# A recommendation tower on one core: the fold of its first layer's weights is moved from the start into the first chunk, in five steps

## The chip, the cores and the metric

The kernel runs on one core of one Trainium2 chip. The metric is the device time of one execution in microseconds.

## The reference

For each of 2048 samples, 32 table rows of 64 numbers are looked up and stacked. Every one of the 496 pairs of fields gives one number, a bilinear form with a matrix of its own; a linear layer takes the 496 numbers to 256, and a small network of three layers follows. All is float32.

```python
e = jnp.stack([tbl_0[ids[:, 0]], ..., tbl_31[ids[:, 31]]], axis=1)   # 2048 x 32 x 64
rows, cols = np.triu_indices(32, k=1)
pij = jnp.einsum('bpe,dpe,bpd->bp', e[:, rows, :], kernel, e[:, cols, :])
z = pij @ W.T + b                                                   # 2048 x 256
h = jnp.concatenate([z, dense_ctx], axis=1)                         # + 16 columns
h = jnp.maximum(h @ W_top1 + b_top1, 0.0)                           # 512
h = jnp.maximum(h @ W_top2 + b_top2, 0.0)                           # 256
y = h @ W_top3
```

## The kernel before

**The fold.** Nothing nonlinear lies between `W` and `W_top1`, so the kernel multiplies the two once and applies the product to the pair sums: `w_comb = W.T @ W_top1[:256]`, and likewise `b_comb = W_top1[:256].T @ b + b_top1`. This is what is called the fold. It has 8 narrow products of one column, which a float32 matmul makes 16 instructions at L401, for the bias, and for each of four groups of rows two products of 128 by 512, four instructions at L406. VectorE moves the results out of PSUM: one addition at L360, and at L368 one copy for each of groups 0 and 1 and four copies of 30 rows for each of groups 2 and 3, whose remaining rows hold the weights of the dense columns. The first use of `w_comb_sb` and `b_comb_sb` is in the layers of chunk 0, which stand in the program among the slots of chunk 1.

**Chunks, turns, slots, sums, layers.** The batch is cut into chunks of 1, 3, 4, 4 and 4 tiles of 128 samples, so the moving side of a matmul is 128, 384 or 512 columns wide. In a chunk:
- GpSimd gathers table rows by indirect DMA (L280), one DMA for each field and tile, 512 in all, in the order chunk, double (a pair of neighbouring fields), field, tile. Double `j` of chunk 0 needs gathers `2j` and `2j + 1`, counted from 0.
- A *turn* transposes a double on TensorE (L431), and ScalarE copies it to `emb_t` (L316).
- A *slot* is a pair of doubles: 16 matmul instructions of 64 by 32 weights (L448) into a pair of PSUM banks, which VectorE multiplies by the other factor into `prod` (L387; L382 and L384 for slots within doubles). There are 128 slots in a chunk, two of them to a *phase*.
- A *sum* adds a quad of blocks of `prod` over partitions: 16 matmul instructions (L468), two phases behind its slots.
- Seven *layer* steps (L494) belong to the chunk before and stand among the slots, from phase 5 on.

**The order.** `program()` writes one list of steps, `PROGRAM`, by hand; every engine walks it and does its own part of each step. It begins with the fold, then the turns of doubles 0 to 3 of chunk 0, then the slots. The further turns of chunk 0 come one phase ahead of the first slot that needs them. The fold waits at its end for `s_folded_out`, that is for VectorE's last copy, before TensorE goes on.

**The ring.** Six PSUM banks are three pairs. Slots, turns and layers take them in turn, in the order of `RING_USES`; `ring_free` makes TensorE wait until the use three before has been read (by VectorE for a slot, by ScalarE for a turn or a layer). The fold writes four banks and one more directly, which is why it has to be out before the ring starts.

**Loads.** ScalarE's queue brings `w_cols` and `W_top1` (semaphore `s_factors`) and then the other weights; the SP queue brings the ids and the 8.2 MB of bilinear matrices in eight pieces. Both are issued in the first ten microseconds.

Of the kernel before, what the change touches and what calls it, by code (L numbers as in the profile page):

```python
# [10 lines left out]
D1 = 256  # L11
H1 = 512
# [42 lines left out]
PROD_BLOCKS = 16  # L55
PROD_QUADS = PROD_BLOCKS // 4
TURNS_AHEAD = 4

SPARE_AT = NQUADS - (NGROUPS - 1) * GROUP_QUADS  # L60
# [65 lines left out]

def program():

    steps = [("fold", 0, 0)]
    steps += [("turn", 0, j) for j in range(TURNS_AHEAD)]  # L130
    for i in range(NCHUNKS):
        for phase in range(NPHASES):
            steps += [("slot", i, s) for s in range(phase * PHASE, (phase + 1) * PHASE)]
            if i == 0:
                turned = [j for j in range(TURNS_AHEAD, DOUBLES) if FIRST_SLOT[j] // PHASE - 1 == phase]
            else:
                turn = TURNS_AHEAD + phase // TURN_EVERY
                turned = [turn] if phase % TURN_EVERY == TURN_EVERY - 1 and turn < DOUBLES else []
            steps += [("turn", i, j) for j in turned]
            turn = (phase - NPHASES) // TURN_EVERY + TURNS_AHEAD  # L140
            if i + 1 < NCHUNKS and phase % TURN_EVERY == TURN_EVERY - 1 and turn >= 0:
                steps.append(("turn", i + 1, turn))
            if phase < SUM_LAG and i > 0:
                late = range(quads_done(NPHASES - 1 + phase - SUM_LAG), quads_done(NPHASES + phase - SUM_LAG))
                steps += [("sum", i - 1, q) for q in late]
            done = range(quads_done(phase - SUM_LAG - 1), quads_done(phase - SUM_LAG))
            steps += [("sum", i, q) for q in done]
            k = (phase - FIRST_LAYER_PHASE) // TURN_EVERY
            if i > 0 and phase % TURN_EVERY == TURN_EVERY - 1 and 0 <= k < NOUTS:
                steps.append(("layer", i - 1, k))  # L150
    steps += [("sum", NCHUNKS - 1, q) for q in range(quads_done(NPHASES - 1 - SUM_LAG), NQUADS)]
    steps += [("layer", NCHUNKS - 1, k) for k in range(NOUTS)]
    return steps
# [2 lines left out]
PROGRAM = program()  # L156

RING_USES = [step for step in PROGRAM if step[0] in ("slot", "turn", "layer")]
RING_USE = {step: n for n, step in enumerate(RING_USES)}  # L160
TURN_USE = {step[1:]: n for n, step in enumerate(step for step in PROGRAM if step[0] == "turn")}

# [10 lines left out]
def build(nc, tables, ids, dense_t, k_slots, w_cols, l0_b, w_top1, b_top1, w_top2, b_top2, w_top3, out):  # L173
# [6 lines left out]
    with ExitStack() as ctx:  # L180
# [169 lines left out]
        @block.vector  # L350
        def _(dve):
            nc.vector.memset(ident[:], 0.0).then_inc(s_consts, 1)
            nc.vector.memset(row_sel[:], 0.0).then_inc(s_consts, 1)
            dve.wait_ge(s_consts, 2)
            nc.vector.memset(row_sel[:, 31:32], 1.0).then_inc(s_consts, 1)

            dve.wait_ge(s_factors, 16 * 4)
            dve.wait_ge(s_folded, 1)
            nc.vector.tensor_tensor(b_comb_sb[:], bilinear[:, NSUMS, 0:H1 // P], b1_sb[:], ALU.add).then_inc(s_folded_out, 1)  # L360
            for at, g in enumerate(reversed(range(NSUMS))):
                dve.wait_ge(s_folded, at + 2)
                if g >= NSUMS - HALVES:
                    parts_out = [slice(32 * b, 32 * b + SPARE_AT) for b in range(4)]
                else:
                    parts_out = [slice(0, P)]
                for rows in parts_out:
                    last = nc.vector.tensor_copy(w_comb_sb[rows, g, :], bilinear[rows, g, :])  # L368
                last.then_inc(s_folded_out, 1)

            def multiply(i, s):
                m, j = SLOTS[s]
                n = cols(i)
                g = i * NSLOTS + s
                bank = ring_bank("slot", i, s)
                quad = i * NQUADS + SLOT_BLOCK[s] // 4
                at = (i * NBLOCKS + SLOT_BLOCK[s]) % PROD_BLOCKS

                wait(dve, s_summed, quad - PROD_QUADS + 1)
                dve.wait_ge(s_bilinear, g + 1)  # L380
                if j is None:
                    nc.vector.tensor_tensor(prod[EMB:P, at, 0:n], bilinear[EMB:P, bank, 0:n],  # L382
                                            emb_t[EMB:P, m - 1, 0:n], ALU.mult)
                    last = nc.vector.tensor_tensor(prod[0:EMB, at, 0:n], bilinear[0:EMB, bank + 1, 0:n],  # L384
                                                   emb_t[0:EMB, m, 0:n], ALU.mult)
                else:
                    last = nc.vector.tensor_tensor(prod[:, at:at + 2, 0:n], bilinear[:, bank:bank + 2, 0:n],  # L387
                                                   emb_t[:, j:j + 1, 0:n].to_broadcast([P, 2, n]), ALU.mult)
                last.then_inc(s_prod, 1)

            for kind, i, which in PROGRAM:
                if kind == "slot":
                    multiply(i, which)

        @block.tensor
        def _(pe):
            def fold():
                pe.wait_ge(s_factors, 16 * 4)
                for m in range(H1 // P):
                    for k in range(D1 // P):  # L400
                        last = nc.tensor.matmul(bilinear[:, NSUMS, m:m + 1], w1_sb[:, k, m * P:(m + 1) * P],  # L401
                                                l0_b_sb[:, k:k + 1], start=k == 0, stop=k == D1 // P - 1)
                last.then_inc(s_folded, 1)
                for g in reversed(range(NSUMS)):
                    for k in range(D1 // P):
                        last = nc.tensor.matmul(bilinear[:, g, :], w_cols_sb[:, k, g * P:(g + 1) * P], w1_sb[:, k, :],  # L406
                                                start=k == 0, stop=k == D1 // P - 1)
                    last.then_inc(s_folded, 1)
                pe.wait_ge(s_consts, 3)
                pe.wait_ge(s_ident, 1)  # L410

                pe.wait_ge(s_folded_out, 1 + NSUMS)

            def ring_free(kind, i, which):

# [4 lines left out]
                if kind == "slot":  # L420
                    pe.wait_ge(s_prod, i * NSLOTS + which + 1)
                elif kind == "turn":
                    pe.wait_ge(s_emb_t, TURN_USE[i, which] + 1)
                else:
                    pe.wait_ge(s_layer_out, i * NOUTS + which + 1)

            def turn(i, j):
                ring_free("turn", i, j)
                pe.wait_ge(s_gathered[j], gathered_count(i))
                for t in range(CHUNKS[i][1]):  # L430
# [43 lines left out]
            def layer(i, k):  # L474
                n = cols(i)
                if i == 0 and k == 0:
                    pe.wait_ge(s_weights, 16 * 11)
                ring_free("layer", i, k)
                if k < H1_OUTS:
                    pe.wait_ge(s_sums_out, (i + 1) * NSUMS)  # L480
# [16 lines left out]

            for kind, i, which in PROGRAM:
                if kind == "fold":
                    fold()  # L500
                elif kind == "turn":
                    turn(i, which)
                elif kind == "slot":
# [49 lines left out]
```

## Time and profile before

| what | value |
|---|---|
| median of 3 runs | 882.09 us (881.82 to 883.49) |
| the profiled execution, its own time | 880.07 us |
| span of the profiled execution | 878.1 us |
| mean granted TensorE clock | 0.996 |
| TensorE busy | 838.8 us (96%) |
| VectorE busy | 632.9 us (72%) |
| GpSimd busy | 483.9 us (55%) |
| ScalarE busy | 71.7 us (8%) |
| fold's matmuls on TensorE | 3.6 us (L401) and 9.4 us (L406) |

### The profile page before, as it was taken

What the parts mean: (1) busy time and instruction counts of PE and PEld (TensorE: products, weight loads), DVE (VectorE), ACT (ScalarE), POOL (GpSimd) and SP (SyncE); (2) the same over time, 40 slices, a digit from 0 to 9 for tenths busy, and PEclk for the clock granted to TensorE, in tenths of its full rate; (3) what the DMA queues carried; (4) which work ended last, traced back from release to release, by engine and by line L of the source; (5) the groups of instructions that cost most, each with busy time, mean ns of one, the idle gap of its engine ahead of it and who ended that gap; (6) DMA issues with size and microseconds to landing.
All of it is one profiled execution on the core that took longest, in us unless ns stands there. A gap on an engine that the chain in (4) does not pass through costs nothing.

```text
span 878.1 us, 33839 instructions
## 1 busy us (share of the span) xinstructions
PE 838.8 (96%) x15748; PEld 346.6 (39%) x15748; DVE 632.9 (72%) x694; ACT 71.7 (8%) x136; POOL 483.9 (55%) x517
## 2 busy tenths in 40 slices
PE   5767899999999999999999999999999999999988
PEld 3545545444443333333333333333333333333333
DVE  3556676799986558999885548999875557999950
ACT  0000011100011110000011110000011111000001
POOL 6777777777777777777777777777720000000000
PEclk9899999999999999999999999999999999999999
DMA  9511111111111111111111111111100000000000
GB/s 333 185 31 30 32 29 30 30 29 31 28 30 28 28 29 28 29 28 29 29 29 29 27 28 29 29 30 28 29 13 2 1 1 2 2 3 2 2 3 0
DMA packets 21597, 29.36 MB, mean 33 GB/s; under 512 B 11121, under 2 KB 11665, under 8 KB 20945
## 3 DMA queue, kind: packets, MB, share of 16 engines
q0 software_dynamic: 16384, 16.81, 10.4%
q1 hardware_dynamic: 3394, 8.79, 2.7%
q8 instruction: 123, 2.02, 0.9%
q10 hardware_dynamic: 1680, 1.61, 0.6%
q14 instruction: 16, 0.13, 0.0%
HBM read 27.17 MB, written 0.01 MB: 31 GB/s over the span
## 4 chain that ended last, share of the span: by engine, by line
PE 94%; issue 3%; DVE 2%; DMA 1%; ACT 0%; SPq 0%; ACTq 0%; DVEq 0%
PE bilinear L448 52%; PE sums L468 26%; PE bilinear L494 11%; PE bilinear L431 4%; DVE w_comb_sb L368 1%; DMA b_sb<-b_top 1%; DVE prod L387 1%; PE bilinear L406 0%; PE bilinear L401 0%; SPq L261 0%; DMA sums_sb<-dense_t 0%; ACTq L298 0%; DVE prod L384 0%; DVE prod L382 0%; DVEq L180 0%
## 5 line engine op out<-in xcount | busy, mean ns | idle before, releaser
L387 DVE TENSOR_TENSOR prod<-bilinear,emb_t 128x1024 f32<-128x1024 f32 (+2 forms) x600 | 579.4, 1006 | 192.5 <-PE bilinear L448 185.3
L280 POOL DMA_INDIRECT emb<-table,ids_sb x512 | 483.4, 944 | 158.7 <-issue 155.3
L448 PE MATMUL bilinear<-emb_t,k_sb 64*32 64x512 f32 (+2 forms) x10240 | 523.2, 507 | 14.1 <-issue 12.0
L448 PEld LDWEIGHTS bilinear<-emb_t,k_sb 64*32 64x32 f32 x10240 | 190.2, 107 | 281.2 <-issue 250.7
L468 PE MATMUL sums<-prod,row_sel 64*32 64x512 f32 (+2 forms) x4960 | 286.6, 508 | 7.7 <-issue 7.3
L468 PEld LDWEIGHTS sums<-prod,row_sel 64*32 64x32 f32 x4960 | 88.7, 107 | 118.1 <-issue 83.0
L316 ACT ACTIVATE emb_t<-bilinear 128x512 f32<-128x512 f32 (+2 forms) x80 | 40.8, 513 | 501.5 <-PE bilinear L431 463.1
L494 PE MATMUL bilinear<-sums_sb,w_comb_sb 128*128 128x512 f32 (+2 forms) x160 | 59.8, 519 | 3.4 <-DMA sums_sb<-dense_t 1.5
L431 PEld LDWEIGHTS bilinear<-ident,emb 128*128 128x128 f32 x256 | 27.3, 141 | 53.2 <-DVE prod L387 47.8
L431 PE MATMUL bilinear<-ident,emb 128*128 128x128 f32 x256 | 45.4, 291 | 1.8 <-DVE w_comb_sb L368 1.6
L494 PEld LDWEIGHTS bilinear<-sums_sb,w_comb_sb 128*128 128x128 f32 x160 | 27.1, 190 | 36.8 <-issue 25.5
L494 PE MATMUL bilinear<-h_sb,w_sb 128*128 128x512 f32 (+5 forms) x100 | 37.6, 517 | 1.7 <-ACT h_sb L332 0.9
L382 DVE TENSOR_TENSOR prod<-bilinear,emb_t 64x512 f32<-64x512 f32 (+2 forms) x40 | 23.5, 588 | 5.8 <-PE bilinear L448 4.7
L494 PEld LDWEIGHTS bilinear<-h_sb,w_sb 128*128 128x128 f32 (+1 forms) x100 | 14.8, 168 | 26.0 <-issue 16.4
L324 ACT ACTIVATE sums_sb<-sums 128x512 f32<-128x512 f32 (+2 forms) x20 | 9.1, 509 | 192.4 <-PE sums L468 192.4
L384 DVE TENSOR_TENSOR prod<-bilinear,emb_t 64x512 f32<-64x512 f32 (+2 forms) x40 | 23.0, 576 | 0.5
L332 ACT ACTIVATE h_sb<-bilinear,b_comb_sb 128x512 f32<-128x512 f32 (+2 forms) x20 | 12.0, 602 | 61.7 <-PE bilinear L494 61.7
L401 PE MATMUL bilinear<-l_b_sb,h_sb 128*128 128x1 f32 x16 | 3.6, 353 | 8.1 <-DMA b_sb<-b_top 8.1
L406 PE MATMUL bilinear<-h_sb 128*128 128x512 f32 x16 | 9.4, 754 | 0.0
L368 DVE COPY w_comb_sb<-bilinear 30x512 f32<-30x512 f32 (+1 forms) x10 | 6.8, 687 | 3.5 <-PE bilinear L406 3.4
L336 ACT ACTIVATE h_sb<-bilinear,b_sb 128x512 f32<-128x512 f32 (+2 forms) x10 | 6.0, 602 | 32.0 <-PE bilinear L494 32.0
L360 DVE TENSOR_TENSOR b_comb_sb<-bilinear,b_sb 128x4 f32<-128x4 f32 x1 | 0.2, 163 | 10.6 <-PE bilinear L401 10.6
(12 smaller groups left out, 12.2 us busy)
## 6 DMA issues: line engine op xcount, KB each, us to landing
emb<-table,ids_sb POOLq DMA_INDIRECT x512
k_sb<-k_slots SPq DMA_DIRECT2D x2, 1088.0 KB, 11.5
k_sb<-k_slots SPq DMA_DIRECT2D x1, 1600.0 KB
k_sb<-k_slots SPq DMA_DIRECT2D x1, 1472.0 KB, 15.0
k_sb<-k_slots SPq DMA_DIRECT2D x1, 960.0 KB, 9.2
k_sb<-k_slots SPq DMA_DIRECT2D x1, 896.0 KB, 20.7
k_sb<-k_slots SPq DMA_DIRECT2D x1, 576.0 KB, 10.4
h_sb<-w_cols ACTq DMA_DIRECT2D x1, 512.0 KB, 4.0
```

The source lines that it names most:

```text
L280: nc.gpsimd.indirect_dma_start(emb[:, j, t, f % 2, :], None, tables[f], bass.IndirectOffsetOnAxis(ap=ids_sb[:, start + t, f:f + 1].bitcast ...
L316: nc.scalar.activation(emb_t[:, j, 0:cols(i)], bilinear[:, ring_bank("turn", i, j), 0:cols(i)], ACT.Copy).then_inc(s_emb_t, 1)
L332: nc.scalar.activation(h1_sb[:, k, 0:n], source, ACT.Relu, bias=b_comb_sb[:, k:k + 1]).then_inc(s_layer_out, 1)
L368: last = nc.vector.tensor_copy(w_comb_sb[rows, g, :], bilinear[rows, g, :])
L382: nc.vector.tensor_tensor(prod[EMB:P, at, 0:n], bilinear[EMB:P, bank, 0:n], emb_t[EMB:P, m - 1, 0:n], ALU.mult)
L384: last = nc.vector.tensor_tensor(prod[0:EMB, at, 0:n], bilinear[0:EMB, bank + 1, 0:n], emb_t[0:EMB, m, 0:n], ALU.mult)
L387: last = nc.vector.tensor_tensor(prod[:, at:at + 2, 0:n], bilinear[:, bank:bank + 2, 0:n], emb_t[:, j:j + 1, 0:n].to_broadcast([P, 2, n]), ...
L406: last = nc.tensor.matmul(bilinear[:, g, :], w_cols_sb[:, k, g * P:(g + 1) * P], w1_sb[:, k, :], start=k == 0, stop=k == D1 // P - 1)
L431: last = nc.tensor.transpose(bilinear[:, ring_bank("turn", i, j), t * P:(t + 1) * P], emb[:, j, t, :, :], ident[:])
L448: last = nc.tensor.matmul(bilinear[col:col + QUARTER, bank + row // EMB, 0:n], k_sb[row:row + EMB, s, col:col + QUARTER], emb_t[row:row + ...
L468: last = nc.tensor.matmul(sums[32 * b:32 * b + 32, half, 0:n], row_sel[rows, 31 - pos:63 - pos], prod[rows, at + b, 0:n], start=pos == 0, ...
L494: last = nc.tensor.matmul(bilinear[0:weights.shape[1], ring_bank("layer", i, k), 0:n], weights, x, start=term == 0, stop=term == LAYER_TER ...
```

## The change

The fold is cut into five steps, `("fold", 0, 0)` to `("fold", 0, 4)`: step 0 makes the bias, steps 1 to 4 one group of rows each (3, 2, 1, 0). They leave the head of the program and stand behind the slots of phases 9, 19, 29, 39 and 49 of chunk 0. Each is a use of the ring like a slot: it waits until its bank pair is free, writes the first bank of it, and the use three behind it waits until VectorE has copied the result. VectorE does the copies where the step stands in the program, between the products of the slots. The wait for VectorE's last copy moves to the first layer step, and the waits for the constants to the first turn.

```diff
+FOLD_EVERY = 10
...
-    steps = [("fold", 0, 0)]
-    steps += [("turn", 0, j) for j in range(TURNS_AHEAD)]
+    steps = [("turn", 0, j) for j in range(TURNS_AHEAD)]
...
+            if i == 0 and phase % FOLD_EVERY == FOLD_EVERY - 1 and phase // FOLD_EVERY <= NSUMS:
+                steps.append(("fold", 0, phase // FOLD_EVERY))
...
-RING_USES = [step for step in PROGRAM if step[0] in ("slot", "turn", "layer")]
+RING_USES = [step for step in PROGRAM if step[0] in ("fold", "slot", "turn", "layer")]
...
-            dve.wait_ge(s_factors, 16 * 4)
-            dve.wait_ge(s_folded, 1)
-            nc.vector.tensor_tensor(b_comb_sb[:], bilinear[:, NSUMS, 0:H1 // P], b1_sb[:], ALU.add).then_inc(s_folded_out, 1)
-            for at, g in enumerate(reversed(range(NSUMS))):
-                dve.wait_ge(s_folded, at + 2)
+            def fold_out(k):
+
+                dve.wait_ge(s_folded, k + 1)
+                source = bilinear[:, ring_bank("fold", 0, k), :]
+                if k == 0:
+                    nc.vector.tensor_tensor(b_comb_sb[:], source[:, 0:H1 // P], b1_sb[:], ALU.add).then_inc(s_folded_out, 1)
+                    return
+                g = NSUMS - k
...
-                    last = nc.vector.tensor_copy(w_comb_sb[rows, g, :], bilinear[rows, g, :])
+                    last = nc.vector.tensor_copy(w_comb_sb[rows, g, :], source[rows, :])
                 last.then_inc(s_folded_out, 1)
+
+            dve.wait_ge(s_factors, 16 * 4)
...
             for kind, i, which in PROGRAM:
-                if kind == "slot":
+                if kind == "fold":
+                    fold_out(which)
+                elif kind == "slot":
                     multiply(i, which)
...
-            def fold():
-                pe.wait_ge(s_factors, 16 * 4)
...
+            def fold(k):
+                ring_free("fold", 0, k)
+                bank = ring_bank("fold", 0, k)
+                if k == 0:
+                    pe.wait_ge(s_factors, 16 * 4)
...
+                else:
+                    g = NSUMS - k
+                    for part in range(D1 // P):
+                        last = nc.tensor.matmul(bilinear[:, bank, :], w_cols_sb[:, part, g * P:(g + 1) * P],
+                                                w1_sb[:, part, :], start=part == 0, stop=part == D1 // P - 1)
                 last.then_inc(s_folded, 1)
...
-                pe.wait_ge(s_consts, 3)
-                pe.wait_ge(s_ident, 1)
-
-                pe.wait_ge(s_folded_out, 1 + NSUMS)
...
+                elif kind == "fold":
+                    pe.wait_ge(s_folded_out, which + 1)
...
             def turn(i, j):
+                if i == 0 and j == 0:
+                    pe.wait_ge(s_consts, 3)
+                    pe.wait_ge(s_ident, 1)
...
                 if i == 0 and k == 0:
                     pe.wait_ge(s_weights, 16 * 11)
+                    pe.wait_ge(s_folded_out, 1 + NSUMS)
```

## Rows read from the trace of the kernel before

**Rows 1.** The page: span, busy time of TensorE, its busy tenths in 40 slices
```profile
span 878.1 us, 33839 instructions
...
PE 838.8 (96%) x15748; PEld 346.6 (39%) x15748; DVE 632.9 (72%) x694; ACT 71.7 (8%) x136; POOL 483.9 (55%) x517
...
PE   5767899999999999999999999999999999999988
```

**Rows 2.** The chain that ended last, in order of time (start us, us, what)
```profile
...
2.26 5.81 DMA b_sb<-b_top
...
28.25 2.66 issue
```

**Rows 3.** Timeline of the first 25 us (start us, us, engine, line, tile, [idle before])
```profile
...
8.11 3.57 PE L401 MATMUL bilinear<-l_b_sb,h_sb 128*128 128x1 f32 x16 [8.11 <-DMA b_sb<-b_top]
...
11.55 9.38 PE L406 MATMUL bilinear<-h_sb 128*128 128x512 f32 x16
...
12.70 0.95 POOL L280 DMA_INDIRECT emb<-table,ids_sb  x1 [0.30 <-issue]
...
15.10 0.34 PEld L406 LDWEIGHTS bilinear<-h_sb 128*128 128x128 f32 x1 [0.52 <-issue]
...
15.35 6.93 DVE L368 COPY w_comb_sb<-bilinear 30x512 f32<-30x512 f32 x10 [3.38 <-PE bilinear L406]
...
16.47 0.19 PEld L406 LDWEIGHTS bilinear<-h_sb 128*128 128x128 f32 x1 [0.24 <-issue]
...
22.54 1.00 PE L431 MATMUL bilinear<-ident,emb 128*128 128x128 f32 x4 [1.61 <-DVE w_comb_sb L368]
...
23.20 0.14 PEld L431 LDWEIGHTS bilinear<-ident,emb 128*128 128x128 f32 x1 [0.39 <-ACT emb_t L316]
...
23.46 0.99 PE L448 MATMUL bilinear<-emb_t,k_sb 64*32 64x128 f32 x48
```

**Rows 4.** Windows: us, busy us of each engine (x instructions), PEclk, DMA share, GB/s
```profile
...
23.46:28.25 4.79, 4.42 (x184) 2.58 (x184) 3.72 (x11) 0.59 (x3) 3.57 (x5) 1.00 0.99 384
30.91:36.60 5.69, 5.32 (x154) 4.03 (x161) 2.96 (x7) 0.42 (x2) 4.17 (x6) 0.50 0.22 53
36.60:41.00 4.40, 4.40 (x233) 3.26 (x225) 2.96 (x9) 0.41 (x2) 3.49 (x4) 1.00 0.18 33
50.00:100.00 50.00, 37.81 (x1767) 27.52 (x1768) 29.14 (x76) 2.17 (x9) 37.75 (x40) 1.00 0.17 31
51.09:54.76 3.67, 2.92 (x128) 1.91 (x128) 1.96 (x5) 0.28 (x1) 2.75 (x4) 1.00 0.16 31
```

**Rows 5.** DMA queues in 50 to 100 us (packets, MB, share of 16 engines)
```profile
...
q8 instruction: 14, 0.23, 1.7%
```

**Rows 6.** Waits from 22.5 to 112 us (us in total, times, longest us)
```profile
...
PE bilinear L448 <- issue: 12.0, 13, 2.7
...
PE sums L468 <- issue: 7.3, 7, 2.1
...
PE bilinear L448 <- DVE prod L387: 1.5, 3, 0.9
```

**Rows 7.** The gathers' DMA queue: whole run, 0 to 18.1 us, 0 to 20.7 us
```profile
...
q0 software_dynamic: 16384, 16.81, 10.4%
...
q0 software_dynamic: 256, 0.26, 4.3%
...
q0 software_dynamic: 321, 0.33, 4.7%
```

**Rows 8.** Timeline: the 128th gather on POOL, and the last turn of chunk 1
```profile
...
162.53 0.95 POOL L280 DMA_INDIRECT emb<-table,ids_sb  x1 [0.30 <-issue]
...
173.46 0.55 PE L431 MATMUL bilinear<-ident,emb 128*128 128x128 f32 x3
```

**Rows 9.** The chain from 99 to 116 us: three transposes with full-size weights
```profile
...
103.71 0.48 PE bilinear L431 x3
```

**Rows 10.** VectorE's copies of the fold: ns min/median/max, first and last start us, forms
```profile
...
L368 DVE COPY w_comb_sb<-bilinear x10: 678/686/697, 15.3 to 21.6; 30x512 f32<-30x512 f32 x8, 128x512 f32<-128x512 f32 x2
```

**Rows 11.** VectorE's products of the one-tile chunk, 22.5 to 112 us, by form
```profile
...
L387 DVE TENSOR_TENSOR prod<-bilinear,emb_t 128x256 f32<-128x256 f32 x120 | 47.5, 422 | 37.2 <-PE bilinear L448 34.2 <-PE sums L468 1.7
```

More of the change, by code:

```diff
@@ L396, in _ @@
         def _(pe):
-            def fold():
-                pe.wait_ge(s_factors, 16 * 4)
[L399 to L402, printed above, removed]
-                last.then_inc(s_folded, 1)
[L404 to L408, printed above, removed]
-                pe.wait_ge(s_consts, 3)
-                pe.wait_ge(s_ident, 1)
-                pe.wait_ge(s_folded_out, 1 + NSUMS)
+            def fold(k):
[3 more added lines that the diff above has]
+                    pe.wait_ge(s_factors, 16 * 4)
+                    for m in range(H1 // P):
+                        for part in range(D1 // P):
+                            last = nc.tensor.matmul(bilinear[:, bank, m:m + 1], w1_sb[:, part, m * P:(m + 1) * P],
+                                                    l0_b_sb[:, part:part + 1], start=part == 0,
+                                                    stop=part == D1 // P - 1)
+                else:
+                    g = NSUMS - k
+                    for part in range(D1 // P):
+                        last = nc.tensor.matmul(bilinear[:, bank, :], w_cols_sb[:, part, g * P:(g + 1) * P],
+                                                w1_sb[:, part, :], start=part == 0, stop=part == D1 // P - 1)
+                last.then_inc(s_folded, 1)
             def ring_free(kind, i, which):
@@ L499, in _ @@
                 if kind == "fold":
-                    fold()
+                    fold(which)
                 elif kind == "turn":
```

## The prediction

> **What bounds the kernel now.** I read the page first. The span is 878.1 us and the tensor engine is busy for 838.8 of them; its busy digits are 9 from the seventh slice on and 5 to 8 in the six slices before [rows 1]. Each slice is 22 us, so the kernel is bound by the tensor engine from about 115 us on, and whatever is to be won or lost lies ahead of that. The chain of waits begins, in order of time, with a DMA until 8.07, goes through the fold's matmuls and meets its longest piece behind them at 28.25, called "issue": the engine waited for nothing that the profile shows [rows 2]. Third, the timeline of the first 25 us. The fold's 16 narrow matmuls begin at 8.11 and take 3.57, its 16 wide ones begin at 11.55 and take 9.38, VectorE's ten copies begin at 15.35 and take 6.93, and the first turn comes at 22.54, released by the last copy; the first slot starts at 23.46 [rows 3]. So the tensor engine does nothing for the chunks in the first 22.5 us.
>
> Last, what bounds the first chunk, into which the fold is moved. Its slots are 128 columns wide. In 50 to 100 us the engine is busy for 37.81 of 50 us, and that stretch saw 14 packets of the instruction queue, one per 3.6 us [rows 4, 5]. A stretch from the end of one "issue" piece to the end of the next took 3.67 us and held 128 matmuls and 128 weight loads [rows 4], and the 14 packets brought 0.23 MB [rows 5], 16.4 KB each: one packet is the 256 instructions of one such stretch. The engine eats its instructions faster than they arrive and stands still once per 256. From 22.5 to 112 us it waited 12.0 us in 13 waits ahead of slots and 7.3 us in 7 ahead of sums for "issue", but only 1.5 us for VectorE's products [rows 6]. The first wait is 2.66 us, at 28.25 [rows 2]; the other 19 share 16.6, or 0.88 us each.
>
> **The change part by part.** It takes the fold off the start, puts one step behind the slots of phases 9, 19, 29, 39 and 49 of the first chunk, lets each use one bank pair of the ring of three, and moves two waits. No DMA is added or moved, and no instruction is added: 32 matmuls, 32 weight loads, one addition and ten copies change places.
>
> *Start.* The turns of doubles 0 to 3 all stand ahead of slot 0, so the first slot needs the gathers of double 3, the seventh and eighth of the run. Every gather is 32 packets (16384 packets for 512 gathers), and 0 to 18.1 us holds 256 packets of that queue, eight gathers [rows 7], although the eighth was issued at 12.70 [rows 3]. So the copies' end stops being the bound at 22.54, and the gathers' landing takes its place: of the 14.4 us that the fold takes in front, only about 5 can be won. From the last turn at 23.20 to the first slot are 0.26 us [rows 3]; with both at the low clock I take 0.4, which puts the first slot at 18.5 where it stood at 23.46: -4.9 us. The next turn, of double 4, needs the tenth gather, and 0 to 20.7 us holds its 320 packets [rows 7]; eight slots and a quad of sums stand ahead of it, 144 matmuls or 2.7 us at the best pace below, so it doesn't wait. At the other end the last turn of chunk 1 stands at 173.46 with its last gather, the 128th, issued at 162.53 [rows 8]: room there too for a head start of 5 us.
>
> *Clock.* The fold also warmed the engine. A weight load of the wide matmuls and the idle time ahead of it make 0.86 us at 15.10 and 0.43 us at 16.47 [rows 3]: the clock went from its 1.2 GHz level to 2.4 GHz near 16.1 (between these two loads), 4.5 us after the wide ones began and 8.0 us after the first narrow one. After the wait at 28.25 the stretch 30.91 to 36.60 ran at a granted clock of 0.50 [rows 4], so it took 5.7 us to come back. Now the first slots start on an idle engine. Pace at the high level is 184 matmuls in 4.79 us, 38.4 per us, and at the low one 154 in 5.69, 27.1 per us [rows 4], so a low microsecond loses 0.29 us. With 5.7 us of it: +1.7 us (1.3 for 4.5 us, 2.3 for 8.0).
>
> *First refill.* The wait of 2.66 us comes after a count of instructions, not at a time, and it is the engine's first. The moved fold lies now behind it and slots lie ahead of it; the wait itself stays, near 27 us, and so does the low stretch behind it: 0. If the engine's idle start let the refill come in time, both would go: -2.66 and 5.7 x 0.29, together -4.3 us. If the low stretches ran into one another, from 18.5 to 36.6 us, that is 18.1 less the wait of 2.66, so 15.4 us at the low clock against the 11.4 counted here and before: +1.2 us.
>
> *The fold's matmuls inside the chunk.* 16 wide ones at 0.43 us make 6.9 us [rows 3]. The narrow ones cost 3.57 us at the low level [rows 3], half of it, 1.8, at the high one if the clock alone sets it; three transposes with the same full-size weights take 0.48 us [rows 9], which makes 2.6 us for 16. I take 2.2. Together +9.1 us (8.7 to 10.5, the latter with the narrow ones still at the low clock).
>
> *VectorE's copies.* They are 0.686 us each in both shapes [rows 10]. Steps 3 and 4 have one copy, which ends before the ring is needed again. Steps 1 and 2 have four, 2.75 us. Queued behind them on VectorE are the products of the next two slots, and the third slot after the step needs the step's banks. Between lie two slots and two quads of sums, 64 matmuls, 1.2 us at the pace of 233 in 4.40 us [rows 4]. So the tensor engine stands for 1.55 us, and while VectorE works off its two products at 0.42 us (47.5 us for 120 [rows 11]) it stays a little behind: 1.7 us each, +3.4 us in all (2.6 to 3.8).
>
> *What hides in the refill waits.* A refill runs while the engine works at a wide matmul or waits for VectorE. A step can save at most the wait of the refill that it covers, 0.88 us on average. Refills come every 127.5 matmuls, counted from the first wait. Counting matmuls in the program's order from there, the steps stand at 0.6, 0.5, 0.3, 0.0 and 0.8 of such a period. Step 3 comes just behind a wait and covers none; the other four lie ahead of one by less than the refill and the sequencer's lead: -3.5 us (-4.4 for all five, -1.5 for few).
>
> The Trainium skill ("Runtime: NRT & Kernel Launch", Instruction fetch mechanics) says that the next block of 256 instructions is fetched while the current one runs and that crossing a block costs little, mostly hidden. The trace agrees with the block's size and not with the hiding: 19.3 us of waits in this chunk. By the page nothing would be there to hide a step in, and the sum would be 3.5 us more.
>
> *Sum.* -4.9 + 1.7 + 9.1 + 3.4 - 3.5 = +5.8 us. The profiled execution took 880.07 us, 2.0 more than its span; it gives 885.9. The median of the runs is 882.09, 2.0 above that execution, so I forecast 882.1 + 5.8 = **887.9 us**. Of the 14.4 us that the fold took in front 9.5 lay in the shadow of the gathers; inside the chunk it costs 9.0 net.
>
> With the bounds: low -4.9 + 1.3 + 8.7 + 2.6 - 4.4 = +3.3, and -1.0 if the first refill's wait goes as well; high -4.7 + 2.9 + 10.5 + 3.8 - 1.5 = +11.0.
>
> **The rivals.**
> *A, the refills set the chunk's pace altogether (faster).* Then only the instruction count matters, which doesn't change, and the fold's work is free: -4.9 + 1.7 = -3.2, 878.9 us. For it speaks the steady 3.6 us per block. Against it: a block has only 0.88 us of waiting, and a step of steps 1 and 2 brings 3.4. It decides once 9.3 of the 12.5 us are hidden, 1.9 per step, over twice the mean wait. Chance 0.07.
> *B, the first refill arrives in time.* The engine is idle until 18 us and its store of instructions is full; the wait of 2.66 us and the clock's fall go: 5.8 - 4.3 = +1.5, 883.6 us. Against it: nothing in the trace makes a refill start before instructions are used up. Chance 0.10; with small errors on top it reaches both sides of "no change".
> *C, the clock stays low longer.* The first refill's wait comes some 8 us after the first turn, so the engine may run low from 18 until 36.6 us, and step 0 then falls into the low stretch: 1.2 us more for the slots and 1.4 for the narrow matmuls: 5.8 + 2.6 = +8.4, 890.5 us. For it: the low level did follow a wait of 2.66 us once. The Trainium skill ("TensorE: Matmul & The Clock Gate", What you observe) has an idle engine start throttled and activity release it; the trace agrees at 16.1 us, and cannot tell whether narrow slots with gaps count as activity as wide matmuls do. Chance 0.15.
> *D, nothing is hidden in the refill waits.* +9.3, 891.4 us: as when a refill starts only once the sequencer has run dry. Chance 0.08.
> The forecast keeps 0.60, with a range of its own of 885.3 to 890.3.
>
> **How the numbers follow.** A measurement of this kernel tells a change from none at about 0.2%, 1.8 us. Slower: the forecast's 0.60, C and D, and a third of B, 0.86. Within 0.2%: half of B and the edge of the forecast, 0.06. Faster: A and a sliver of B, 0.08. The range of 8 in 10 leaves out A, the lower half of B and the far ends of C and D: 883.5 to 892.5 us.
>
> **What would show it.** The first slot near 18.5 us, with the seven or eight gathers' landing as what it waited for; weight loads or slots at a granted clock of 0.5 in the first microseconds after it; an "issue" wait of some 2.7 us near 27 us; four wide matmuls of 1.7 us in all at steps 1 to 4; waits of the tensor engine of 1.5 us for VectorE's copies or the product behind them twice, near 52 and 68 us; and the start of chunk 1's own slots some 6 us later than now. It is wrong if the first slot comes before 17 us or after 20, if the idle time by "issue" in the first chunk falls by more than 5 us, or if the end of chunk 0 and the end of the run move by different amounts.

## The result, and the profile after

The changed kernel is slower: 885.05 us in the median of 20 runs, against 882.21 for 20 runs of the kernel before. The ratio is 1.0039, with a 95% interval of 1.0025 to 1.0052, so +3.4 us (2.2 to 4.6). The forecast was +5.8 us, 887.9 us. The profiled execution took 884.15 us with a span of 882.2, 4.1 above the span of before [rows 1].

The page of the changed kernel:

```profile
span 882.2 us, 33840 instructions
...
PE 840.1 (95%) x15748; PEld 346.2 (39%) x15748; DVE 633.3 (72%) x694; ACT 72.0 (8%) x136; POOL 484.0 (55%) x517
...
PE   2878899999999999999999999999999999999988
...
PEclk9799999999999999999999999999999999999999
```

Against [rows 1] the first slice has fallen from 5 to 2 and the next four are 8, 7, 8, 8 where they were 7, 6, 7, 8: work has left the start and is spread over the first chunk. The sixth slice is 9 in both, and from there on nothing has changed.

The chain that ended last, for the start and the first refill:

```profile
12.67 5.82 DMA emb<-table,ids_sb
...
18.63 0.45 PE bilinear L444
...
25.05 2.60 issue
```

The eighth gather's landing has taken the place of the fold: it was issued at 12.67, and the fourth turn begins at 18.63. The long wait of [rows 2] has moved from 28.25 to 25.05 us and is as long as it was, 2.60 against 2.66 us. It does come after a count of instructions: the windows from the start of the span to that wait hold 219 and 220 matmuls, and 220 weight loads each. The row of before, then that of the changed kernel:

```profile
0.00:28.25 28.25, 18.01 (x219) 10.28 (x220) 10.96 (x25) 2.45 (x6) 19.16 (x25) 1.00 0.95 347
```

```profile
0.00:25.05 25.05, 7.78 (x220) 5.25 (x220) 4.44 (x15) 2.67 (x6) 16.72 (x22) 1.00 0.96 341
```

The timeline of the changed kernel, TensorE and VectorE at steps 0 and 1, and TensorE behind the copies of steps 1 and 2:

```profile
34.98 2.01 PE L412 MATMUL bilinear<-l_b_sb,h_sb 128*128 128x1 f32 x16
...
51.17 3.19 PE L418 MATMUL bilinear<-h_sb 128*128 128x512 f32 x4
...
54.40 2.79 DVE L372 COPY w_comb_sb<-bilinear 30x512 f32<-30x512 f32 x4 [2.87 <-PE bilinear L418]
...
57.24 0.91 PE L461 MATMUL bilinear<-emb_t,k_sb 64*32 64x128 f32 x32 [1.62 <-DVE w_comb_sb L372]
...
71.69 0.91 PE L461 MATMUL bilinear<-emb_t,k_sb 64*32 64x128 f32 x32 [1.71 <-DVE w_comb_sb L372]
```

The 16 narrow matmuls take 2.01 us at the high clock. Step 1's four wide ones take 3.19, because they fall into a low stretch of the clock. For the copies of steps 1 and 2 TensorE stands still for 1.62 and 1.71 us.

Windows of the changed kernel (columns as in [rows 4]; the column before the last two is the granted clock), first the stretch behind the first slot, then one at the high clock and two low ones:

```profile
19.00:23.28 4.28, 4.28 (x146) 3.52 (x145) 2.82 (x8) 0.28 (x1) 3.37 (x4) 1.00 1.02 405
...
33.52:36.93 3.41, 3.41 (x96) 2.98 (x95) 1.57 (x4) 0.00 (x0) 2.50 (x4) 0.97 0.15 31
36.93:40.34 3.41, 3.41 (x118) 2.80 (x119) 1.29 (x4) 0.28 (x1) 2.50 (x4) 0.53 0.13 27
...
50.58:54.00 3.42, 3.42 (x21) 1.28 (x5) 0.79 (x2) 0.28 (x1) 2.50 (x4) 0.53 0.14 31
```

The 1.00 of the first of these rows is no reading: the record of the clock in this trace begins near 23.1 us. What tells the level there is the weight load of a turn, 0.18 us at 18.60 and 0.14 at 23.16; at 28.65, where the clock was granted at 0.50, it takes 0.18 again:

```profile
18.60 0.18 PEld L444 LDWEIGHTS bilinear<-ident,emb 128*128 128x128 f32 x1 [2.22 <-issue]
...
23.16 0.14 PEld L444 LDWEIGHTS bilinear<-ident,emb 128*128 128x128 f32 x1 [0.36 <-issue]
...
28.65 0.18 PEld L444 LDWEIGHTS bilinear<-ident,emb 128*128 128x128 f32 x1 [0.38 <-issue]
```

Waits of TensorE in the first chunk, 18.5 to 116.5 us (us in total, times, longest us), to be held against [rows 6]:

```profile
PE bilinear L461 <- issue: 9.9, 11, 2.6
...
PE bilinear L461 <- DVE w_comb_sb L372: 3.3, 2, 1.7
...
PE sums L481 <- issue: 2.0, 3, 0.8
```

The waits for instructions are 11.9 us in 14 pieces, where they were 19.3 in 20. Without the first, long one, 16.6 us have become 9.3. This is where the forecast's error lies.

Nearly all the difference has arisen by the end of the first chunk: a turn near it stands at 116.44 us, where it stood at 112.49. The last turn of chunk 1 stands at 177.66 us, 4.2 later than in [rows 8], and the span is 4.1 longer:

```profile
177.66 0.55 PE L444 MATMUL bilinear<-ident,emb 128*128 128x128 f32 x3
```

### The profile page after: what moved, and what is told of

Same layout as the page of the kernel before. It is cut to its first block, busy times and chain, and to the rows that moved or that the text cites. A ratio compares the mean times of both kernels' runs of the same rounds, so it can differ in the third digit from the quotient of the medians.

```text
span 882.2 us, 33840 instructions
## 1 busy us (share of the span) xinstructions
PE 840.1 (95%) x15748; PEld 346.2 (39%) x15748; DVE 633.3 (72%) x694; ACT 72.0 (8%) x136; POOL 484.0 (55%) x517
## 4 chain that ended last, share of the span: by engine, by line
PE 94%; issue 2%; DMA 1%; DVE 1%; POOL 1%; ACT 0%; SPq 0%; DVEq 0%; POOLq 0%
PE bilinear L461 52%; PE sums L481 26%; PE bilinear L508 11%; PE bilinear L444 4%; PE bilinear L418 1%; POOL emb L282 1%; DMA emb<-table,ids_sb 1%; DVE w_comb_sb L372 0%; DVE prod L393 0%; PE bilinear L412 0%; SPq L263 0%; DMA sums_sb<-dense_t 0%; DVEq L182 0%; ACT sums_sb L326 0%; DVE prod L390 0%
## 5 line engine op out<-in xcount | busy, mean ns | idle before, releaser
L418 PEld LDWEIGHTS bilinear<-h_sb 128*128 128x128 f32 x16 | 3.2, 223 | 3.1 <-issue 2.9
L342 ACT ACTIVATE y_sb<-bilinear 1x512 f32<-1x512 f32 (+2 forms) x5 | 2.5, 501 | 9.2 <-PE bilinear L508 9.2
```

What stands on the lines that cost most here:

```text
L418: last = nc.tensor.matmul(bilinear[:, bank, :], w_cols_sb[:, part, g * P:(g + 1) * P], w1_sb[:, part, :], start=part == 0, stop=part == D1 ...
```

## The experiments

The question after the result was why a fold that costs 14 us of work and waiting inside the chunk made the kernel only 3.4 us slower. The tally theory says: each term as in the prediction, only with more hidden in the refill waits. The rivals say that the place or kind of a step does not matter, or that the low clock is what costs.

One thing has to be known to read the numbers. In 10 of the 12 runs every kernel, the kernel before included, took about 1370 to 1400 us, since TensorE's instructions followed one another several times slower for much of the time; what that looks like stands in the last section. I call it the late condition. The ratios to the kernel before are given, but they are ratios in that condition and don't test the prediction's terms. Two runs, step0_front and hybrid_third, had the usual pace of 882 us.

**One copy in each step.** All 128 rows of the result are copied at once; the dense columns' weights are not loaded.

```diff
...
-                if g >= NSUMS - HALVES:
-                    parts_out = [slice(32 * b, 32 * b + SPARE_AT) for b in range(4)]
-                else:
-                    parts_out = [slice(0, P)]
+                parts_out = [slice(0, P)]
...
```

Expected of one_copy:

> The changed kernel with one copy of 128 rows in every step, where steps 1 and 2 have four of 30; the eight small loads of the dense columns' weights into those rows are left out, so the dense columns are weighted with numbers of the fold. Tally theory (a step costs its matmuls and the wait for VectorE, less at most one refill wait): the two waits for the copies, 3.3 us in the changed kernel's trace, go, and since the wide matmuls cover the refill by themselves nothing is given back: 2.6 to 3.3 us faster than the changed kernel, about even with the kernel before. Rival (the refills set the pace, and any delay of under a few us in a block is mostly free): under 1.5 us faster than the changed kernel.

**The same with the steps just behind a refill wait (one_copy_lit), and inside the time of a refill (one_copy_shade).** The edit of the first; the second has the phases (9, 22, 30, 41, 49).

```diff
-FOLD_EVERY = 10
+FOLD_PHASES = (9, 23, 31, 39, 47)
...
-            if i == 0 and phase % FOLD_EVERY == FOLD_EVERY - 1 and phase // FOLD_EVERY <= NSUMS:
-                steps.append(("fold", 0, phase // FOLD_EVERY))
+            if i == 0 and phase in FOLD_PHASES:
+                steps.append(("fold", 0, FOLD_PHASES.index(phase)))
...
```

Expected of one_copy_lit:

> As one_copy, with the steps behind phases 9, 23, 31, 39 and 47: by the count of matmuls steps 1 to 4 then come within a tenth of a block behind a refill wait. Same arithmetic as one_copy. Tally theory: none of the four covers a refill, where in one_copy three do: 2 to 3 us slower than one_copy, waits for issue in the first chunk larger by as much. Rival (a step covers whatever refill comes next, wherever it stands, because the sequencer runs ahead): within 0.7 us of one_copy.

Expected of one_copy_shade:

> As one_copy, with the steps behind phases 9, 22, 30, 41 and 49: steps 1 to 4 come 0.65 to 0.85 of a block behind a refill wait, inside the time of the refill. Tally theory: all four cover one: 0.5 to 1 us faster than one_copy and 3 to 3.5 us faster than one_copy_lit. Rival (place does not matter): within 0.7 us of both.

**Steps 1 to 4 left out (no_wide).**

```diff
-            if i == 0 and phase % FOLD_EVERY == FOLD_EVERY - 1 and phase // FOLD_EVERY <= NSUMS:
+            if i == 0 and phase % FOLD_EVERY == FOLD_EVERY - 1 and phase // FOLD_EVERY == 0:
...
+                    last = nc.vector.memset(w_comb_sb[rows, g, :], 0.01)
...
```

Expected of no_wide:

> The changed kernel without steps 1 to 4: the 16 wide matmuls and the copies are left out and the folded weights are a constant, written by VectorE before the first slot. Tally theory: it takes away 6.9 us of wide matmuls and 3.3 us of waits for copies and gives back 3 to 4 us of refill waits: 6.5 to 7.5 us faster than the changed kernel, about 878.5 us. Rival (most is hidden in refill waits): 2 to 4 us faster than the changed kernel. Rival (low clock is what the change costs): 4 to 5 us, with the granted clock's mean as in the kernel before.

Measured, all four on one chip and in the late condition, with the kernel before at 1389.5 us: one_copy 1398.6 (ratio 1.0055, 1.0027 to 1.0083), one_copy_lit 1397.1 (1.0055, 1.0034 to 1.0076), one_copy_shade 1400.9 (1.0099, 1.0068 to 1.0130), no_wide 1390.3 (1.0006, 0.9984 to 1.0028). The trace of one_copy shows why these don't answer the question; its waits over the whole span are nearly nine times those of the kernel before, which has all of its 19.3 us in the first chunk [rows 6]:

```profile
PE bilinear L454 <- issue: 147.4, 217, 2.4
...
PE sums L474 <- issue: 22.0, 51, 1.0
```

Two things can be read, for this condition only. The placement that should cover four refills was slower than the one that should cover none, or even with it (the intervals overlap), and not 3 us faster. And leaving out steps 1 to 4 was faster than one copy in each, by some 7 us, with intervals that just touch. What either is worth at the usual pace these runs don't say.

**Steps 1 to 4 left out, repeated**, to get the number at the usual pace. Expected of steps_gone, steps_gone_again and steps_gone_third, in this order:

> The same kernel as in run no_wide (the changed kernel without steps 1 to 4: the 16 wide matmuls and the copies are left out, the folded weights are a constant), once more, since its first run came from a chip on which TensorE's instructions arrived several times slower in all kernels. Tally theory: 6.5 to 7.5 us faster than the changed kernel, about 877.5 to 878.5 us, 0.4 to 0.5% faster than the kernel before. Rival (refill waits hide most of the steps): 2 to 4 us faster than the changed kernel, so about 881 to 883 us.

> The changed kernel without steps 1 to 4 (the 16 wide matmuls and the copies are left out, the folded weights are a constant). From the changed kernel's trace steps 1 to 4 take 8.5 us of TensorE and 3.3 us of its waiting for the copies, and the chunk's issue waits shrank by 7.4 us. Tally theory with the measured sizes: about 5 us faster than the changed kernel, so 2 us faster than the kernel before. With the sizes of the prediction: 7.5 us faster than the changed kernel. Rival (the low clock at the start and after step 0 is the main cost): under 3 us faster than the changed kernel.

> The changed kernel without steps 1 to 4 (the 16 wide matmuls and the copies are left out, the folded weights are a constant), for a chip at the usual pace. In the changed kernel's trace steps 1 to 4 take 8.5 us of TensorE and 3.3 us of its waiting for copies. Tally theory with the measured sizes (a refill wait is given back for nearly all that a step adds to its block, about 6 us in all): 5 to 6 us faster than the changed kernel, 2 to 3 us faster than the kernel before. With the sizes of the prediction (one refill wait of 0.88 us for each of three steps): 7.5 to 9 us faster than the changed kernel, 4.5 to 6 us faster than the kernel before. Rival (what costs time is step 0 and the low clock at the start, not steps 1 to 4): under 3 us faster than the changed kernel, even with the kernel before or slower.

None of the three had the usual pace: 1.0028 (1.0006 to 1.0049), 1.0032 (1.0012 to 1.0053) and 1.0007 (0.9990 to 1.0024). One copy, repeated beside the second of them (one_copy_again), gave 1.0054 (1.0030 to 1.0077). Expected of it:

> The changed kernel with one copy of 128 rows in each step (the dense columns' weights are not loaded). Tally theory: the two waits of the tensor engine for the four copies, 3.3 us in the changed kernel's trace, go and little is given back: 2.6 to 3.3 us faster than the changed kernel, even with the kernel before within 1 us. Rival (a refill runs during such a wait, so that what is won there is given back at the next refill): under 1.5 us faster than the changed kernel.

Over these runs the kernel without steps 1 to 4 is at or slightly above the kernel before although its first slot comes over 4 us earlier (19.01 to 19.12 us in the three traces): in the late condition the earlier first slot did not show in the time. None of these eight runs with fewer, shorter or moved steps tells the theories apart, so the main question was not answered by an experiment. The price of steps 1 to 4 and of the copies at the usual pace was not measured.

**Step 0 back in front**, a run at the usual pace:

```diff
-    steps = [("turn", 0, j) for j in range(TURNS_AHEAD)]
+    steps = [("fold", 0, 0)]
+    steps += [("turn", 0, j) for j in range(TURNS_AHEAD)]
...
-            if i == 0 and phase % FOLD_EVERY == FOLD_EVERY - 1 and phase // FOLD_EVERY <= NSUMS:
+            if i == 0 and phase % FOLD_EVERY == FOLD_EVERY - 1 and 1 <= phase // FOLD_EVERY <= NSUMS:
```

Expected of step0_front:

> The changed kernel with step 0 (the bias, 16 narrow matmuls) back at the head of the program, where the engine has nothing else to do until the gathers land; steps 1 to 4 stay among the slots. Tally theory: the narrow matmuls' 2.0 us leave the chunk, and with them the low stretch of the clock that followed them in the changed kernel's profile (36.9 to 40.3 us at half clock, in which the narrow matmuls are what the engine had just done); less what is given back in refill waits: 2 to 3 us faster than the changed kernel, even with the kernel before within 1 us. Rival (step 0 is covered by refill waits like the others): under 1 us faster than the changed kernel. On a chip where TensorE's instructions arrive several times slower, all of it vanishes in the waits for them: within 0.2% of the kernel before.

Measured: 884.3 us beside 882.55, a ratio of 1.0028 (1.0014 to 1.0043). The changed kernel had 1.0039 (1.0025 to 1.0052): 1.0 us better by the middles, with intervals that overlap. The tally theory's 2 to 3 us did not come, nor was the kernel even with the one before; the number is that of the rival, by which step 0 in the chunk is covered by refill waits like the others. The windows of its profile bring a second reason:

```profile
27.90:31.30 3.40, 3.03 (x99) 2.16 (x83) 1.87 (x5) 0.28 (x1) 2.65 (x3) 0.54 0.97 375
34.70:41.50 6.80, 6.18 (x209) 4.86 (x203) 3.48 (x9) 0.28 (x1) 4.97 (x7) 0.52 0.15 30
72.20:75.60 3.40, 3.40 (x143) 3.25 (x144) 2.51 (x7) 0.00 (x0) 2.48 (x4) 0.55 0.13 27
```

There are three low stretches, 13.6 us together, although step 0 is gone from the chunk. Two follow refill waits of 2.05 and 1.89 us, the third a wait of 1.8 us for the copies of step 2. So the expectation that the low time goes with step 0 fell. In the changed kernel the stretch of 36.93 to 40.34 us had no wait over 0.4 us in the 9 us ahead of it, only step 0; whether the narrow matmuls brought on that one stays open.

**The fold in front, under the gathers.** A version put together from both kernels: steps 0 to 3 between the first turns, none waiting at once for its copies, ScalarE making two of the four copies of steps 1 and 2, step 4 behind phase 31.

```diff
-FOLD_EVERY = 10
+FOLD_LATER = {31: 4}
...
-    steps = [("turn", 0, j) for j in range(TURNS_AHEAD)]
+    steps = [("fold", 0, 0), ("turn", 0, 0), ("fold", 0, 1), ("turn", 0, 1), ("fold", 0, 2), ("turn", 0, 2), ("fold", 0, 3), ("turn", 0, 3)]
...
+            def fold_out(k):
+                act.wait_ge(s_folded, k + 1)
+                g = NSUMS - k
+                for b in range(2, 4):
+                    rows = slice(32 * b, 32 * b + SPARE_AT)
+                    last = nc.scalar.activation(w_comb_sb[rows, g, :], bilinear[rows, ring_bank("fold", 0, k), :],
+                                                ACT.Copy)
+                last.then_inc(s_folded_act, 1)
...
```

Expected of hybrid, hybrid_again and hybrid_third, in this order:

> A kernel put together from both: steps 0 to 3 stand in front, between the turns 0 to 3 as their gathers land, each using the ring and none waiting for its copies at once; step 4 stands behind phase 31. ScalarE makes two of the four copies of steps 1 and 2. Tally theory: the engine is idle until 18.2 us for the gathers anyway, so steps 0 to 3 are free there and warm the clock; the first slot starts near 19.3 us instead of 23.46 (-4.2), step 4 costs 1.7 less up to 0.9: 3 to 3.5 us faster than the kernel before, 878.6 to 879.1 us. Rival (what the start gains is lost in refill waits, which come by the count of instructions): within 1.5 us of the kernel before. Rival (the clock's low stretches come by chance): a spread of several us between runs as in the changed kernel, and no more than 2 us gained in the median.

> The kernel of run hybrid once more, since its first run came from a chip on which TensorE's instructions arrived several times slower. Steps 0 to 3 in front between the turns, step 4 behind phase 31, ScalarE makes half of the 30-row copies. Tally theory: first slot near 19.3 to 20.2 us (it was 20.15 in the first run, in which the engine still ran at its usual pace until then) instead of 23.46, step 4 costs 1.7 less up to 0.9: 2.4 to 3.5 us faster than the kernel before. Rival (what the start gains is lost in refill waits): within 1.5 us of the kernel before.

> The kernel of run hybrid a third time, for a chip at the usual pace. Steps 0 to 3 in front between the turns, step 4 behind phase 31, ScalarE makes half of the 30-row copies. Tally theory: first slot near 20.2 us instead of 23.46 in the kernel before and 19.0 in the changed one, no waits for the fold's copies in the chunk, step 4 for 1.7 us less up to 0.9: 2.4 to 3.3 us faster than the kernel before, 5 to 6 us faster than the changed kernel. Rival (what the start gains is lost in refill waits, which come by the count of instructions): within 1.5 us of the kernel before. Rival (the clock's low stretches by themselves make the changed kernel slow): 2 to 3 us faster than the changed kernel and a granted clock above its 0.992.

The first two runs fell into the late condition, at 1.0017 (0.9993 to 1.0041) and 1.0010 (0.9989 to 1.0031). The third had the usual pace: 882.28 us beside 883.07, a ratio of 0.9992 (0.9973 to 1.0010). That is even with the kernel before, and about 4 us faster than the changed kernel by the two ratios. The start went as meant; the chain of its profile:

```profile
12.25 3.41 PE bilinear L430 x4
15.66 0.21 PE bilinear L458
15.88 2.31 PE bilinear L430 x4
18.19 0.11 PE bilinear L458
18.30 1.73 PE bilinear L430 x4
...
20.05 0.70 DVE w_comb_sb L384
...
25.23 2.89 issue
```

The wide steps stand one behind another with turns between, the first slots run from 20.05 and, after a short wait for a copy, from 20.89. The first refill comes 3 us earlier than in the kernel before. But of these 3 us less than 1 reached the end (0.7 by the middle of the ratio; the two profiled executions even differ by 1.0 the other way, 879.1 against 878.1 us). The waits and the low stretches of the clock say where they went:

```profile
PE bilinear L475 <- issue: 13.6, 13, 2.9
...
PE sums L495 <- issue: 4.9, 6, 1.4
```

```profile
26.90:37.20 10.30, 8.42 (x240) 6.63 (x248) 4.00 (x10) 0.56 (x2) 7.86 (x9) 0.51 0.53 188
50.80:57.60 6.80, 6.46 (x223) 4.70 (x207) 4.03 (x10) 0.28 (x1) 5.04 (x6) 0.52 0.15 29
```

The waits for instructions are 18.5 us, nearly the 19.3 of [rows 6]; the clock was low for 17 us, against 5.7 to 7 us around the one low stretch of [rows 4]. Its mean granted clock was 0.990. An estimate from these rows: 3.0 us from the start, step 4's 1.9 against them, 0.8 fewer of waits, and some 10 more low microseconds at 0.29 each make +1.1 us, and the spans differ by +1.0. By this estimate the refill waits that the steps hid in the changed kernel are back, and the low clock took what the start gained. The tally theory's 2.4 to 3.3 us did not come, the number is that of the first rival (within 1.5 us). The second rival, that the low clock alone makes the changed kernel slow, wanted a clock above 0.992; it was 0.990, and the kernel still 4 us faster than the changed one.

## Why the prediction was right, and where a term was off

The direction held, and so did the start, the first refill, the copies and the places of the steps; the time lay in the range of 8 in 10, 883.5 to 892.5 us, just below the forecast's own of 885.3 to 890.3, and 2.4 us below the forecast in the difference. One step of the mechanism failed: how much a step hides. The prediction had set its own sign for that, an idle time by "issue" that falls by more than 5 us, and it fell by 7.4. The 3.8 us too little there were partly made up by costs set too low or not forecast, 2.8 us together (matmuls and low stretches). That the time came out as near as it did is in part luck. In the profiled pair the terms can be measured one by one.

| term | forecast | measured in the trace |
|---|---|---|
| first slot, 23.46 to 19.00 | -4.9 | -4.5 |
| low clock behind the first slot | +1.7 | +1.1 |
| length of the first refill wait | 0 | -0.1 |
| fold's matmuls in the chunk | +9.1 | +10.7 |
| waits for VectorE's copies | +3.4 | +3.3 |
| further low stretches | 0 | about +1.2 |
| hidden in the other refill waits | -3.5 | -7.3 |
| sum | +5.8 | +4.4; the span has +4.1 |

*Start.* Right. The gathers, not the fold, bound the first slot once the fold was gone; of 14.4 us of fold in front only 4.5 came free. The turns took a little longer at the low clock than I had put.

*Clock.* The mechanism was right, the size a little less. From the first slot to the turn of double 4 are 3.04 us in the kernel before (23.46 to 26.50) and 4.16 in the changed one (19.00 to 23.16). The Trainium skill ("TensorE: Matmul & The Clock Gate", What's actually happening) has an idle engine start throttled. The trace agrees: 146 matmuls in the 4.28 us behind 19.00, against 184 in 4.79 [rows 4], and the turn's weight load at 0.18 us until then.

*First refill.* Right: same count, same length.

*Matmuls.* 1.94 us on the chain for step 0 (forecast 2.2), and 2.98, 1.92, 1.91 and 1.92 for steps 1 to 4 (forecast 1.7 each). The excess of 1.1 us in step 1 is a low stretch of the clock at 0.53, after a refill wait of 1.82 us.

*Further low stretches.* Not forecast. In 36.93 to 40.34 us the granted clock was 0.53 and the pace 118 matmuls in 3.41 us, 34.6 per us, where the kernel before ran 233 in 4.40, 53 per us [rows 4]: some 1.2 us, if nothing else had held that stretch up. But over whole blocks the kernel before makes only 35 per us (1767 in 50 us [rows 4]), so part of it would have been lost in refill waits anyway. Rival C had the low clock last longer right behind the start; it came in pieces instead.

*VectorE's copies.* Right in size and kind, 1.6 and 1.7 us.

*Hidden in refill waits.* This is the step that failed: "A step can save at most the wait of the refill that it covers, 0.88 us on average." Five steps took away 7.3 us, 1.5 each, past the forecast's bound of 4.4 for all five. The number of waits fell from 20 to 14, so six went for five steps, and those left are shorter as well (9.3 us for 13, 0.72 each, against 0.88). So a step hides more than the refill that it covers. The changed kernel's own trace shows it at steps 3 and 4, which have one copy each and lie at the high clock; the chain, then the windows between two waits:

```profile
81.31 0.83 issue
...
82.54 1.91 PE bilinear L418 x4
...
89.74 0.84 issue
...
93.17 0.86 issue
...
96.42 1.92 PE bilinear L418 x4
...
103.90 0.68 issue
```

```profile
82.14:89.74 7.60, 7.60 (x255) 4.75 (x255) 4.40 (x11) 0.28 (x1) 5.77 (x7) 1.00 0.15 30
94.03:103.90 9.87, 9.86 (x382) 6.59 (x382) 6.66 (x16) 0.56 (x2) 7.43 (x9) 1.00 0.18 32
```

Step 3 stands just behind a wait, where by the rule it covers none; yet the next wait comes 255 matmuls later, two blocks and not one. Step 4 is followed by a wait only after three blocks, so two waits went for one step. Its three blocks take 10.55 us with the wait behind them, 3.5 each, no more than the 3.6 that a block takes in the kernel before: here the step was free, as rival A has it. The trace of step0_front shows the same two gaps, 255 and 382 matmuls, the second with a pause of 0.15 us in it and at 3.8 us for a block. So a step hides waits even where it does not stand ahead of a refill; refills seem to go on during a step, and what they get ahead by lasts for the blocks behind it. That is read from two traces and was not tested by moving a step at the usual pace. Steps 1 and 2 take 4.6 and 3.6 us with their waits for the copies, as long as a block or longer, and the low stretches run at a pace that the refills keep up with; how the 7.3 us divide between these was not separated. The placements that should have done it ran in the late condition. The Trainium skill ("Runtime: NRT & Kernel Launch", Instruction fetch mechanics) would have such refills mostly hidden; the trace has waits of 19.3 us before and 11.9 after.

*The clock and the spread.* The 20 runs of the changed kernel reach from 882.75 to 889.2 us, and the granted clock goes with it: the ten runs at 0.994 or 0.996 average 883.8 us, the eight at 0.990 or below 887.5. Counting low time as twice one minus the clock times the span, it is 14.0 us on average against 8.7 in 25 runs of the kernel before, and a fit over the changed kernel's runs gives 0.29 us more for each low microsecond, the size that the prediction took from [rows 4]. The low time right behind the start is not in it, since the record begins only after it. So about 1.5 of the 3.4 us go with more time at the low clock. A run with more low time may also have had more waits for another reason, so this is a correlation, not shown as cause.

*The rivals.* A (free inside the chunk) is out for the five steps together, which used up the head start and 4 us more; it holds near step 4. B is out, since the first refill's wait stayed. D is out, since more was hidden than forecast, not less. C did not come as it was put: the clock was up near 23.1 us and step 0 ran at the high level, 2.01 us; other low stretches cost 1 to 2 us.

*A reading.* The prediction has the busy digits at 9 from the seventh slice on; in [rows 1] they are 9 from the sixth, 110 us. Nothing hangs on it. The high end of its sum starts from -4.7 us, a number it doesn't derive; with -4.9 the end would be +10.8.

## What to carry to other kernels

Before work is moved out of the start, look for what is late next: here gathers that landed at 18 us covered most of the fold, so the move could win only 4.5 of 14.4 us, and the work then stood in a place where it cost some 7 and went with more time at the low clock. Short matmuls can be bound by the arrival of their instructions, with one wait per 256; long ones put between them are partly free, so price such a move by the waits of the whole chunk and not one refill for each step. And what a start does in the shadow of a load is better left there: the version that did so was 4 us faster than the changed kernel, though only even with the kernel before.

## What the hardware did unexpectedly

In ten runs TensorE's instructions followed one another so slowly that all kernels took 1370 to 1400 us. It is not the refill wait of this document: in the row of one_copy below 7 matmuls and 7 weight loads start in 20 us, with no packet of the instruction queue q8 in that time, and the single waits are 2.4 us long. It goes with GpSimd's gathers. In the first run of the hybrid, windows with the gathers running and with GpSimd idle (columns as in [rows 4]):

```profile
475.00:500.00 25.00, 25.00 (x621) 14.85 (x613) 23.80 (x29) 0.87 (x2) 0.00 (x0) 1.00 0.01 3
...
550.00:575.00 25.00, 21.58 (x187) 6.19 (x188) 7.18 (x9) 1.19 (x2) 14.30 (x16) 0.86 0.10 19
750.00:775.00 25.00, 25.00 (x477) 15.22 (x467) 23.55 (x23) 1.08 (x2) 0.00 (x0) 1.00 0.01 2
```

One_copy, with the gathers running:

```profile
40.00:60.00 20.00, 2.57 (x7) 0.86 (x7) 0.00 (x0) 0.00 (x0) 15.12 (x16) 1.00 0.14 27
```

While GpSimd is busy, 187 matmuls pass in 25 us; while it is idle, 621 and 477. At the usual pace the gathers run as well and no such thing is seen: 480 matmuls in 400 to 425 us of the kernel before, with GpSimd busy for 18.9 us. The chip of hybrid_third, at the usual pace, had the condition in one_copy and the three runs beside it and in steps_gone_third, so it is not the chip alone; what sets the condition stays open.

Also unexpected: the clock's low stretches are not a fixed part of a program. The same kernel ran with a mean of 0.985 in one execution and 0.996 in another, 5 us apart.

One execution of the kernel before, beside step0_front, took 1695.4 us at a mean clock of 0.961. It is left out of the ratio, and nothing here says what happened in it.
